# Two spectral convolution layers on one core: layer 1's first product in 64x64 tiles of TensorE, and an inverse operand of 90 columns in place of 128

## The reference

```
# layer 0, per image; 23 of the 46 half-spectrum columns are kept
f = fft2(x, axes=(1, 2), norm='ortho');  Xk = (f.real - f.imag)[:, :, :23]      # 8 blocks of 48 channels
o1 = relu(einsum('bhwni,nio->bhwno', Xk, w1[0]) + b1[0])
o2 = softshrink(einsum(o1, w2[0]) + b2[0], 0.01)
x  = ifft2(o2 padded with zeros).real + x
# layer 1
xr, xi = rfft2(x).real, rfft2(x).imag                                          # the same 23 columns
o1r = relu(xr @ w1[0] - xi @ w1[1] + b1[0]);  o1i = relu(xi @ w1[0] + xr @ w1[1] + b1[1])
o2r = softshrink(o1r @ w2[0] - o1i @ w2[1] + b2[0]);  o2i = softshrink(o1i @ w2[0] + o1r @ w2[1] + b2[1])
y  = irfft2(o2r + 1j * o2i padded) + x
```

## Time and profile before

| what | value |
|---|---|
| median of 3 runs | 525.07 us (524.0 to 528.05) |
| the profiled execution, its own time | 527.67 us |
| its span, first to last instruction | 525.8 us |
| mean granted TensorE clock | 0.969 of 2.4 GHz |
| PE / PEld busy | 480.0 us (91%) / 347.5 us (66%) |
| DVE / ACT / POOL busy | 303.9 / 208.8 / 172.8 us |

### The profile page before, as it was taken

The page is one execution under the profiler, slowest core; times in us unless marked ns, Lnnn a source line. Parts: engine busy times, 40 slices in busy tenths (PEclk is TensorE's granted clock), DMA queues, the critical chain, the costliest instruction groups (busy, mean ns, idle before and its releaser), DMA issues.

```text
span 525.8 us, 14875 instructions
## 1 busy us (share of the span) xinstructions
PE 480.0 (91%) x6144; PEld 347.5 (66%) x6144; DVE 303.9 (58%) x674; ACT 208.8 (40%) x473; POOL 172.8 (33%) x194
## 2 busy tenths in 40 slices
PE   4549999999999999999999999999999999998772
PEld 1137777767777677767777676777777777876531
DVE  6413456456764577456764577456763677566642
ACT  0014544554354433554354433454345433433101
POOL 9703133113432134313442133312442123222124
PEclk9858999999999999999999999999999999999967
DMA  8859955476899588877889688886989565735397
GB/s 187 268 141 218 272 149 150 105 205 181 253 222 244 154 210 246 238 202 184 263 216 236 173 208 242 228 213 176 255 221 248 167 175 156 156 84 141 108 242 223
DMA packets 76720, 104.65 MB, mean 199 GB/s; under 512 B 7761, under 2 KB 63303, under 8 KB 76526
## 3 DMA queue, kind: packets, MB, share of 16 engines
q1 hardware_dynamic: 57622, 55.97, 39.8%
q0 software_dynamic: 10608, 40.45, 29.1%
q10 hardware_dynamic: 8424, 7.28, 5.5%
HBM read 52.23 MB, written 51.43 MB: 197 GB/s over the span
## 4 chain that ended last, share of the span: by engine, by line
PE 79%; DMA 6%; DVE 6%; POOL 3%; ACT 2%; issue 2%; SPq 1%; ACTq 0%; POOLq 0%; DVEq 0%
PE ps L605 13%; PE ps L669 13%; PE ps L694 12%; PE ps L656 11%; PE ps L572 10%; PE ps L618 9%; PE ps L681 5%; PE ps L634 4%; DMA scr_f<-fs 3%; PE ps L644 3%; DVE img L551 2%; DVE ns L525 2%; ACT p L442 1%; POOL img L386 1%; POOL xs L369 1%
## 5 line engine op out<-in xcount | busy, mean ns | idle before, releaser
L551 DVE TENSOR_TENSOR img<-ps,img 90x768 f32<-90x768 f32 x92 | 82.7, 900 | 23.0 <-PE ps L605 18.1
L369 POOL TENSOR_TENSOR xs<-xs,nt 128x360 f32<-128x360 f32 (+1 forms) x48 | 41.5, 865 | 149.3 <-DVE nt L503 121.7
L605 PE MATMUL ps<-jr,cst 64*128 64x384 f32 (+1 forms) x358 | 83.6, 535 | 7.2 <-DVE img L551 5.7
L572 PE MATMUL ps<-img,cst 128*64 128x384 f32 (+1 forms) x368 | 72.2, 506 | 12.4 <-DMA img<-x 7.6
L378 POOL DMA_DIRECT2D y<-img x42 | 34.6, 825 | 136.0 <-DVE img L551 135.6
L618 PEld LDWEIGHTS ps<-cst,bt 128*64 128x64 f32 x1472 | 63.2, 141 | 21.0 <-issue 13.9
L435 ACT ACTIVATE o<-ps,wt 97x180 f32<-97x180 f32 (+1 forms) x96 | 33.8, 405 | 107.2 <-PE ps L656 107.1
L618 PE MATMUL ps<-cst,bt 128*64 128x90 f32 x1472 | 69.0, 248 | 6.7 <-DMA bt<-scr_f 6.7
L525 DVE SCALAR_TENSOR_TENSOR ns<-p,ps 109x384 f32<-109x384 f32 x96 | 53.2, 554 | 37.9 <-ACT p L442 33.0
L669 PE MATMUL ps<-wt,o 128*64 128x96 f32 x1472 | 73.9, 250 | 0.5 <-DVE o L517 0.5
L669 PEld LDWEIGHTS ps<-wt,o 128*64 128x64 f32 x1472 | 64.9, 137 | 12.6 <-issue 12.6
(11 more groups left out here) (41 smaller groups left out, 411.5 us busy)
## 6 DMA issues: line engine op xcount, KB each, us to landing
y<-img POOLq DMA_DIRECT2D x35, 540.0 KB, 5.5
img<-x POOLq DMA_DIRECT2D x30, 540.0 KB, 8.5
scr_i<-et SPq DMA_DIRECT2D x48, 270.0 KB, 5.7
scr_f<-fs SPq DMA_DIRECT2D x176, 72.0 KB, 3.4
bt<-scr_f SPq DMA_DIRECT2D x40, 270.0 KB, 4.6
jr<-scr_i SPq DMA_DIRECT2D x48, 216.0 KB, 5.1
img<-x ACTq DMA_DIRECT2D x10, 540.0 KB, 7.4
y<-img SPq DMA_DIRECT2D x11, 270.0 KB, 3.8
```

The costliest lines, as they stand in the source:

```text
L369: nc.gpsimd.tensor_tensor(re, re, nt[s % 2][:, :, 0:kws(s), 0:H], ALU.subtract).then_inc(re_ok, 1)
L551: nc.vector.tensor_tensor(y, p, y, ALU.add).then_inc(i_add, 1)
L572: last = mm(ps[64 * r:64 * r + 64, P3 + g % 2, 0:(b - a) * HC], K["w_fwd"], img[t % IMGS][:, a:b, :].rearrange("p h c -> p (h c)"), start= ...
L605: last = mm(ps[:, B0 + r, 0:n], K["w_inv"][64 * r:64 * r + 64, :], set_rows(t, j)[64 * r:64 * r + 64, at, 0:n], start=True, stop=True)
```

## The change

`c1` is split by output: for each (q, im, ab) there are now two matmuls (o = 0 real, o = 1 imaginary), each 64x64, into partitions 64 o to 64 o + 63. So `w1` is laid out in 128 columns per operand (48 real, 16 zeros, 48 imaginary, 16 zeros), `w21`, `bias1` and `sign` move the imaginary half to rows 64 and up, the row that carries the bias becomes row 48, and relu reads 112 partitions in place of 97. DVE's preparation of `w21` is two operations on 112 partitions x 384 in place of one on 96 x 384 and one on 1 x 768. `w_inv` loses its 38 columns of zeros, so an inverse matmul loads 90 columns and writes 90 partitions.

```diff
-    put("w_inv", np.concatenate([rows, np.zeros((2 * KW, 128 - W))], 1), 0, 64)
+    put("w_inv", rows, 0, 64)
...
-    sign[BS:2 * BS] = -1
+    sign[64:64 + BS] = -1
...
-WCOLS = {"w10": HALVES * 2 * 64, "w20": HALVES * 2 * 64, "w1": 2 * HALVES * 2 * (2 * BS + 1), "w21": NBLK * 2 * BS,
+WCOLS = {"w10": HALVES * 2 * 64, "w20": HALVES * 2 * 64, "w1": 2 * HALVES * 2 * 128, "w21": NBLK * 2 * BS,
...
-            w21[2 * BS, n, i * BS:(i + 1) * BS] = l1_b2[i, n]
-            w["bias1"][i * BS:(i + 1) * BS, n] = l1_b1[i, n]
+            w21[BS, n, i * BS:(i + 1) * BS] = l1_b2[i, n]
+            w["bias1"][64 * i:64 * i + BS, n] = l1_b1[i, n]
             for o in range(2):
-                w1[64 * ab:64 * ab + BS, i, n // 2, o * BS:(o + 1) * BS] = l1_w1[i ^ o, n]
-                w21[i * BS:(i + 1) * BS, n, o * BS:(o + 1) * BS] = l1_w2[i ^ o, n]
+                w1[64 * ab:64 * ab + BS, i, n // 2, 64 * o:64 * o + BS] = l1_w1[i ^ o, n]
+                w21[64 * i:64 * i + BS, n, o * BS:(o + 1) * BS] = l1_w2[i ^ o, n]
...
# relu of c1, on ACT (L435) and alike on DVE (L517)
-                        nc.scalar.activation(o11[0:2 * BS + 1, 2 * q, 0:kws(s), 0:H],
-                                             ps[0:2 * BS + 1, P2, q * STEP * H:q * STEP * H + n].rearrange("p (k m) -> p k m", m=H), ACT.Relu, bias=bias1[0:2 * BS + 1, b:b + 1]).then_inc(c1_act, 1)
+                        nc.scalar.activation(o11[0:64 + BS, 2 * q, 0:kws(s), 0:H],
+                                             ps[0:64 + BS, P2, q * STEP * H:q * STEP * H + n].rearrange("p (k m) -> p k m", m=H), ACT.Relu, bias=bias1[0:64 + BS, b:b + 1]).then_inc(c1_act, 1)
...
# preparation of w21, on DVE
-                    v = w21[0:2 * BS, :, 0:BS]
-                    nc.vector.tensor_scalar(v, v, K["sign"][0:2 * BS, :], None, ALU.mult).then_inc(w_ok, 1)
-                    v = w21[2 * BS:2 * BS + 1, :, :]
-                    nc.vector.tensor_scalar(v, v, LAM, None, ALU.add).then_inc(w_ok, 1)
+                    v = w21[0:64 + BS, :, 0:BS]
+                    nc.vector.tensor_scalar(v, v, K["sign"][0:64 + BS, :], K["lam"][0:64 + BS, :], ALU.mult, ALU.add).then_inc(w_ok, 1)
+                    v = w21[0:64 + BS, :, BS:2 * BS]
+                    nc.vector.tensor_scalar(v, v, K["lam"][0:64 + BS, :], None, ALU.add).then_inc(w_ok, 1)
...
# inv, on TensorE (L605)
-                        last = mm(ps[:, B0 + r, 0:n], K["w_inv"][64 * r:64 * r + 64, :], set_rows(t, j)[64 * r:64 * r + 64, at, 0:n], start=True, stop=True)
+                        last = mm(ps[0:W, B0 + r, 0:n], K["w_inv"][64 * r:64 * r + 64, :], set_rows(t, j)[64 * r:64 * r + 64, at, 0:n], start=True, stop=True)
...
# c1, on TensorE (L656)
                             for ab in range(2):
-                                k = slice(64 * ab, 64 * ab + 64)
-                                last = mm(ps[0:2 * BS + 1, P2 + ab, q * STEP * H:q * STEP * H + n], w1[k, im, 2 * f + q, :],
-                                          xt[k, q, 0:kws(s), im * H:(im + 1) * H], start=im == 0, stop=im == 1)
+                                for o in range(2):
+                                    k, m = slice(64 * ab, 64 * ab + 64), slice(64 * o, 64 * o + 64)
+                                    last = mm(ps[m, P2 + ab, q * STEP * H:q * STEP * H + n], w1[k, im, 2 * f + q, m],
+                                              xt[k, q, 0:kws(s), im * H:(im + 1) * H], start=im == 0, stop=im == 1)
```

More of the change, by code:

```diff
@@ L80, in weights @@
     w10, w20 = w["w10"].reshape(128, HALVES, 2, 64), w["w20"].reshape(128, HALVES, 2, 64)
-    w1, w21 = w["w1"].reshape(128, 2, HALVES * 2, 2 * BS + 1), w["w21"].reshape(128, NBLK, 2 * BS)
+    w1, w21 = w["w1"].reshape(128, 2, HALVES * 2, 128), w["w21"].reshape(128, NBLK, 2 * BS)
     bias0 = w["bias0"].reshape(128, HALVES, 2)
-    bias0[:], w["bias1"][:] = 1.0, 1.0
+    bias0[:], w["bias1"][BS] = 1.0, 1.0
     for n in range(NBLK):
@@ L516, in _ @@
                         dve.wait_ge(c1_mm, 2 * s + 2)
-                        nc.vector.tensor_scalar(o11[0:2 * BS + 1, 2 * q + 1, 0:kws(s), 0:H],
-                                                ps[0:2 * BS + 1, P2 + 1, q * STEP * H:q * STEP * H + n].rearrange("p (k m) -> p k m", m=H),
-                                                bias1[0:2 * BS + 1, b:b + 1], 0.0, ALU.add, ALU.max).then_inc(c1_dve, 1)
+                        nc.vector.tensor_scalar(o11[0:64 + BS, 2 * q + 1, 0:kws(s), 0:H],
+                                                ps[0:64 + BS, P2 + 1, q * STEP * H:q * STEP * H + n].rearrange("p (k m) -> p k m", m=H),
+                                                bias1[0:64 + BS, b:b + 1], 0.0, ALU.add, ALU.max).then_inc(c1_dve, 1)
                 if kind == "d1":
```

## The result

The changed kernel takes 530.34 us (median of 13 runs, 528.34 to 531.45) against 526.31 us for the kernel before in the same comparison (13 runs): a ratio of 1.0072, 95% interval 1.0056 to 1.0088. On 526.3 us that is +3.8 us (+2.9 to +4.6). The forecast was +4.5 us. All ratios here go by the runs that lie within 1.5% of the fastest run of their kernel; only experiment 4 has others (522.59 and 522.88 us, two of its six), which count in its median and its spread but not in its ratio.

What follows compares the result with a forecast made beforehand. TensorE's order of work was taken as the bound. `c1` and neighbours +5.8, inverse operand -1.8 and start +0.5 gave +4.5 us, or 529.6 us on the median of 525.07, range 526.0 to 534.0.

Steps and rivals of the forecast that it cites:

- Rounds: In `c1`: 8 rounds before and after, each still 0.155 us, so nothing gained in streaming.
- Rival 1: In `c1`: four tiles don't hide their weight loads, +14.4 us more than the forecast, 544.0 us; chance 0.12.
- Changes of shape: Between TensorE stages of different tile shape: array empties, first load unhidden; 0.16 us with 64 columns, about 0.17 with 90.
- rival 2: Around `c1`: 64x64 tiles follow 64x128 tiles without a gap, -2.2 us in sum, 522.9 us; chance 0.08.
- some 0.09 us: Where the tile shape changes on TensorE: the time the array takes to run empty, before the first weight load.
- Which neighbour pays: Stages around the 48 `c1`: cost set by neighbours, such as +0.17 us at `e`, +0.16 at `c1` behind an inverse group.
- six `c1` with 135 columns: Between two inverse groups, the second waiting for DVE's add: the added change of shape costs nothing.
- c1 term: All 48 `c1` with their neighbours, changes of shape gained and lost: together +5.8 us.
- two groups counted as covered: Of nine `c1` between `t` and an inverse group, two hidden by longer DVE waits; seven pay 0.15, +1.05 us.
- The inverse operand: Inverse groups with unhidden first loads: 90 columns load faster than 128, 0.03 us each, -1.8 us.
- The start: Loading of weights at the kernel's start: 108 KB more at about 230 GB/s, +0.5 us.
- The first c1: The first `c1`, standing before `c0`, which then has its tile shape: -0.16 us.

Runs made afterwards that it cites:

- experiment 4: The changed kernel with `e` and `inv` also in 64x64 tiles, operands padded to 128 columns; ratio 0.9818 against the kernel before, median 518.88 us.
- experiment 5: The changed kernel with `e` also in 64x64 tiles and `inv` left in 64x128; ratio 1.0087 against the kernel before.
- experiment 6: The changed kernel with `c1` as one 64x128 matmul per operand in place of two column tiles; ratio 0.9981 against the kernel before.
- experiment 3: The kernel before with 248 unused columns added to the weights loaded at the start; ratio 0.9993 against the kernel before.
- experiment 1: The changed kernel with the inverse operand back at 128 columns; ratio 1.0116 against the kernel before.

## Why the prediction was right, point by point

The range of 526.0 to 534.0 us alone tests little: its lower end lies at the time of the kernel before, 526.31 us in the comparison. What was tested is the lengths of the stages, which repeat to about 0.01 us where nothing waits.

- **Rounds.** Forecast: 8 rounds of 0.155 us in four tiles as in two. Measured: 1.24 us for 32 instructions where no change of shape is in front (experiment 4), 1.40 behind `t`, which is what was written. Rival 1 wanted 1.7 us. The page that it leaned on (the Trainium skill, "TensorE: Matmul & The Clock Gate", section The mechanism: loads overlap matmuls only when the row group differs) does not hold here: eight rounds of four tiles, two in each row half, show no unhidden load after the first. What was forecast beside it, PE's busy time "about as before", did not come: it rose by 5.8 us, 5.0 of them between the second `c1` and the last `c0`.
- **Changes of shape.** Forecast: 0.17 us at `e`, 0.16 us at a `c1` behind an inverse group. Measured: 0.17 and 0.16. No row of before had shown the way from 64x64 to 64x128; it costs what the others cost, and rival 2 is out. The Trainium skill, "TensorEngine Tiling (Array Packing)", section Key Properties, says that changing the mode drains the array while changing the tile doesn't; experiments 4 and 5 agree in both halves. Together with the first load the price is 0.16 us with 64 columns to load, 0.17 with 90, 0.18 with 97 and 0.20 with 128 (experiment 6: 1.44 less 1.24). How much of it is the running empty alone, the prediction's "some 0.09 us", no run here separates.
- **Which neighbour pays.** The step with inverse groups was to grow by 0.10 us: +0.16 at `c1`, nothing behind it, 0.03 back at two groups. From inverse group to inverse group of the next step it grew from 9.23 us (258.97 - 249.74) to 9.32 (261.99 - 252.67). The six `c1` with 135 columns were to cost nothing: from the inverse group in front to the one behind it was 1.99 us (258.97 to 260.96) and is 1.96 (261.99 to 263.95). The c1 term as a whole, +5.8 us, measured +6.1 (+4.8 to +7.4) with the start in it.
- **The two groups counted as covered.** This step of the prediction was wrong, and small. From the start of `c1` to the start of `e`, over the inverse group between, the nine places behind `t` took 1.96 us in the profile before (the last, with 135 columns, 1.65) and take 2.12 in the changed one (1.81), 0.16 us more; one there has 2.23. The exceptions before were two places with 2.99 and 2.27 us. The first:

```profile
169.55 1.49 PE L656 MATMUL ps<-xs,wt 64*97 64x180 f32 x16
171.82 0.92 PE L605 MATMUL ps<-jr,cst 64*128 64x384 f32 x4 [0.78 <-ACT fs L408]
```

It waits for ACT behind a slow store, not for DVE's add, and in the profile of experiment 3 this place has 1.96 us. Such waits come and go between profiles. So all nine pay, and the term is 0.3 us larger than counted.
- **The inverse operand.** Forecast -1.8 us, measured -2.2 (-3.2 to -1.2). The groups behind `c1` that I counted into other terms (12 times 0.03 us) would be the rest, but the interval holds both.
- **The start.** +0.5 us were taken from the bytes. The load does take 0.5 us longer, but whether that reaches the end is open: experiment 3 gives -0.4 us (-1.4 to +0.7). The sum is +4.5 with the term and +4.0 without it, and both lie in the measured +2.9 to +4.6. The prediction's sign, a first `c0` later than 36.1 us, came (36.7 us), but a single profile doesn't carry it: with the larger weights that start lies anywhere from 35.9 to 37.2 us.
- **The fit of the sum.** Each measured term is known to 1 us or so, so that the total is within 0.7 us of the forecast is partly luck. The steps are not: +0.15 and +0.09 us where +0.15 and +0.10 were forecast.
- **The first c1.** It was to gain 0.16 us from standing beside `c0`. It shares the shape, but it runs at a granted clock of 0.50 (1.2 GHz), and when that rises to 2.4 GHz differs between profiles. The busy times by stretch (us of the stretch, PE, PEld, DVE, ACT, POOL, then the granted clock as a share of 2.4 GHz, DMA's share and GB/s) show it reached in the kernel before by 42.5 us, while its first `c1` ends, and in the changed kernel hardly begun at 44:

```profile
42.50:43.00 0.50, 0.50 (x14) 0.23 (x10) 0.12 (x1) 0.12 (x1) 0.00 (x0) 1.00 1.04 263
```

```profile
43.50:44.00 0.50, 0.50 (x12) 0.40 (x8) 0.00 (x0) 0.00 (x0) 0.00 (x0) 0.50 0.91 217
44.00:44.50 0.50, 0.50 (x16) 0.34 (x8) 0.07 (x1) 0.07 (x1) 0.00 (x0) 0.57 1.04 249
```

In the timelines the first `c1` takes 2.24 us before, 2.68 us in the changed kernel, 2.45 in experiment 1 and 1.91 in experiment 5. The term of 0.16 can't be seen under that.

What stays open: by experiment 3 the start's cost is only known to within 2 us, and the price of a change of shape isn't split into the running empty and the first load.

## What to carry to other kernels

Read the shape of the tiles of each stage on TensorE together with the order of the stages: here a stage of 8 short rounds pays 0.16 to 0.18 us, more than a tenth of itself, when its neighbour has another shape. Splitting an operand into column tiles doesn't shorten a stream that each tile must have in full (1.24 us for `c1` either way); in these runs it paid only where it made neighbours equal. Here `c1` split, without the shorter inverse operand, cost 1.2%, and the same split carried through `inv` and `e`, so that four stages share one shape, makes the kernel 1.8% faster than before (at least 1.4% by the interval): experiment 4 beats both kernels.

## What had not been expected

The sizes fitted; two things about reading single profiles had not been expected. Profiles with the same, larger weights put the first `c0` anywhere from 35.9 to 37.2 us, and in experiment 3 a start 1.6 us later went with a span 1.3 us shorter, because waits elsewhere and the end of the kernel differ between profiles too. Comparing step by step, where the lengths repeat, avoids that. And experiment 4's runs spread over 8.7 us (514.15 to 522.88) where those of the changed kernel spread over 3.1; its profile happens to be the fastest of its runs, so its span of 512.4 us is not the one to quote. Why it spreads more was not tried.
